# Expert gate weights fetched from DRAM per tile instead of copied in SBUF, and two PSUM banks for tile results

## The chip, the cores and the metric

The kernel runs on one core of one Trainium2 chip. The metric is the time of one execution in microseconds of device time, lower is better. Three runs of the kernel before are given; one further execution was profiled.

## The reference

The input is `x` of shape (16, 256, 128), all in float32. Four blocks follow each other, each adding to `x`; the two mixture-of-experts blocks have the same weights.

```
x = x + attn_a(layernorm(x))      # causal, 16 heads of 8
x = x + ffn(layernorm(x))
x = x + attn_b(layernorm(x))      # scaled by norms, 16 heads
x = x + ffn(layernorm(x))

def ffn(x):                        # D=128, HIDDEN=512, 8 experts, top 2
    logits = flat_x @ Wr
    top_vals, top_idx = top_k(logits, 2)
    rw = softmax(top_vals)
    combine = sum(rw[..., None] * one_hot(top_idx, 8), axis=1)
    g = einsum('nc,ech->neh', flat_x, Wg)
    u = einsum('nc,ech->neh', flat_x, Wu)
    h = silu(g) * u
    eo = einsum('neh,ehc->nec', h, Wd) / sqrt(12)
    out = einsum('ne,nec->nc', combine, eo)
```

## The kernel before

The program is written out by hand for each engine, and semaphores join the five instruction streams; nothing is reordered by a scheduler. Each stream runs attention A, the expert tiles of layer 0, attention B, and the expert tiles of layer 1.

**The expert tiles.** The 4096 tokens, each with two experts, are sorted by expert: a routing step on VectorE gives every (token, choice) pair a row of the DRAM tensor `xg`, in which each expert begins at a multiple of 128 rows. That makes at most `TILES` = 71 tiles of 128 rows per layer. GpSimd scatters the normalised tokens `xn` into `xg` with indirect DMAs (line 1214) and later gathers the results from `eo` (line 1227). The tokens are routed in two groups; the second group's routing and scatters run beside the first tiles, in pieces that `pe_route`, `act_route` and `dve_route` place ahead of tile `k`. The constants `ROUTE_...` say at which `k`: LN at 0, T 1, LG 2, PICK 3, CNT 4, SUM 5, BASE 6, SLOT 7, and two more pieces at 8 and 9. The last one fills the table `te` with the expert of each tile.

**One iteration `k` of `tile_loop`, engine by engine.** TensorE (`pe_tile`): g of tile k (line 1331, four 128x128 matmuls into `psS`), u of tile k (line 1338, into `psT`), the transpose T of tile k+1 (line 1321), y of tile k-1 (line 1350, four matmuls into `psN`). ScalarE (`act_tile`): a copy of the u weights of tile k+1 (`wuc`), silu of g into `sg`, a copy of the transposed tile into `xTt` (line 1366). VectorE (`dve_tile`): the copy of tile k-2's result from `psN` into `ysb` (line 1395), the copy of tile k+1's gate weights into `wgc` (line 1388), the product `hT` of tile k (line 1402). SyncE (`sp_tile`): the load of `xin` for tile k+2 once T of tile k is done (line 1415), the store of `ysb` of tile k-2 (line 1419). A tile's weights lie in SBUF for all eight experts (`wg`, `wu`, `wd`, loaded during attention A); an engine that needs an expert's slice reads its column from `te` into a register first (line 1298, `expert`).

GpSimd makes the `wgc` copies of the first `POOL_COPIES` = 9 tiles of each layer (line 1239), VectorE those of the other 62.

What sets the order around the change is the text of these functions, and the waits in them. `f_sem` counts finished pieces by tile: y of tile k-1 waits for `F_y` of the tile before it, that is for the copy that empties the single bank `psN`:

```
after(pe, f["h"], n0 + k)
if k == 1:
    pe.wait_ge((LA, LB)[l].s["x1"], NBLK)
after(pe, f["y"], n0 + k - 1)
```

The last ten iterations of layer 0 also hold first steps of attention B (`AHEAD_...`). Behind some iterations VectorE combines the gathered results into `x` and starts the next normalisation (`dve_behind`).

## Time and profile before

| | us |
|---|---|
| runs shown: median, lowest, highest | 1279.55, 1272.09, 1284.77 |
| the profiled execution's own time | 1278.22 |
| its span, from first to last instruction | 1276.4 |
| tile loop of layer 0, first to last `xTt` copy | 368.7 to 595.1 |
| tile loop of layer 1, first to last `xTt` copy | 1005.1 to 1221.1 |

Engines are named PE (TensorE matmul), PEld (its weight load, which overlaps), DVE (VectorE), ACT (ScalarE), POOL (GpSimd) and SP (SyncE); a name with a q behind it is that engine's sequencer, and SPq rows are DMA issues. A float32 matmul of 128x128 stands in the rows as two instructions, so the four matmuls of g are x8. "psS<-xTt,wgc" reads: writes psS, reads xTt and wgc. Times count from the span's start. In square brackets stands how long the engine was idle before a row, and what released it.

### The profile page before, as it was taken

To read this page: it belongs to the slowest core of one execution; us is meant where nothing else is said; L and a number is where in the kernel's file an instruction comes from. 1 tells how busy PE (TensorE), PEld (TensorE's weight loads), DVE (VectorE), ACT (ScalarE), POOL (GpSimd) and SP (SyncE) were. 2 spreads that over 40 slices of the span, in tenths; PEclk is the share of its full clock that TensorE was granted. 3 is DMA by queue.
4 is the path that set the end of the run, shared out by engine and by line. 5 is a ranking of instruction groups with operands and counts; after the bars stand their busy time and mean duration, and the time that the engine had idled before them with its cause. 6 is when DMAs were issued, how large, how long until landed. Compare 5 with 4: busy or idle time off the path is not lost.

```text
span 1276.4 us, 29420 instructions
## 1 busy us (share of the span) xinstructions
PE 1067.0 (84%) x9198; PEld 732.0 (57%) x9198; DVE 816.1 (64%) x2452; ACT 673.3 (53%) x1399; POOL 551.6 (43%) x1028
## 2 busy tenths in 40 slices
PE   3988999887788999998788889998867789999940
PEld 1344555443377899887334344443522689999940
DVE  5677778867646445657667888888674464445622
ACT  2465777643433455454276678887645434555520
POOL 2233444325823611444777545454635135014335
PEclk9998999886659999999577799998856789999975
DMA  5585444632101212222433323333201012122222
GB/s 158 118 212 136 102 103 119 172 107 50 39 23 53 83 56 57 72 72 78 109 82 101 81 66 89 89 91 77 52 23 41 22 55 82 55 59 80 72 82 67
DMA packets 163006, 104.80 MB, mean 82 GB/s; under 512 B 15397, under 2 KB 156201, under 8 KB 162857
## 3 DMA queue, kind: packets, MB, share of 16 engines
q1 hardware_dynamic: 154664, 86.14, 26.1%
q0 software_dynamic: 8192, 16.79, 4.6%
q8 instruction: 79, 1.29, 0.5%
q14 instruction: 71, 0.57, 0.2%
HBM read 52.74 MB, written 50.14 MB: 81 GB/s over the span
## 4 chain that ended last, share of the span: by engine, by line
PE 64%; DVE 17%; issue 9%; POOL 3%; ACT 2%; another core or an unknown queue 2%; DMA 2%; SPq 1%; ACTq 0%; DVEq 0%; POOLq 0%
PE psS L1331 10%; PE psT L1338 9%; PE psO L309 8%; PE psN L1350 8%; PE psS L343 7%; DVE mx L655 4%; PE psS L370 3%; PE psT L351 3%; PE psM L267 3%; PE psM L1321 2%; PE psN L316 2%; PE psN L325 1%; PE psO L945 1%; PE psM L410 1%
## 5 line engine op out<-in xcount | busy, mean ns | idle before, releaser
L655 DVE TENSOR_REDUCE mx<-psS 128x3 f32<-128x384 f32 (+1 forms) x512 | 311.9, 617 | 138.5 <-PE psS L370 67.1
L343 PE MATMUL psS<-kst,qst 48*128 48x256 bf16 (+1 forms) x1024 | 205.5, 290 | 57.5 <-DVE mx L655 44.3
L542 ACT ACTIVATE pT<-psT,scb 128x512 f32<-128x512 f32 x256 | 194.7, 778 | 74.0 <-PE psT L351 42.8
L351 PE MATMUL psT<-qst,kst 50*128 50x256 bf16 (+1 forms) x1024 | 198.9, 286 | 9.6 <-ACT pT L542 4.5
L1214 POOL DMA_INDIRECT xg<-xn,slot x128 | 124.0, 969 | 112.8 <-DVE slot L1177 29.5
L1350 PE MATMUL psN<-wd,hT 128*128 x1136 | 153.8, 279 | 18.6 <-DVE ysb L1395 16.6
L1331 PE MATMUL psS<-xTt,wgc 128*128 128x128 f32 x1136 | 157.2, 282 | 12.6 <-ACT xTt L1366 6.9
L771 POOL TENSOR_SCALAR_AFFINE_SELECT pT<-pT 128x256 f32<-128x256 f32 x256 | 103.9, 413 | 142.2 <-ACT pT L537 140.6
L1402 DVE TENSOR_TENSOR hT<-sg,psT 128x512 f32<-128x512 f32 x142 | 97.5, 686 | 105.3 <-PE psT L1338 83.6
L343 PEld LDWEIGHTS psS<-kst,qst 48*128 48x128 bf16 x1024 | 67.4, 97 | 157.9 <-DVE mx L655 79.2
L309 PE MATMUL psO<-pT,vp 128*32 128x256 f32 (+1 forms) x2048 | 152.3, 425 | 5.6 <-POOL pT L771 5.6
L537 ACT ACTIVATE pT<-psT 128x384 f32<-128x384 f32 x256 | 122.5, 490 | 60.4 <-PE psT L351 55.8
L1338 PE MATMUL psT<-xTt,wuc 128*128 128x128 f32 x1136 | 153.3, 279 | 0.0
L1350 PEld LDWEIGHTS psN<-wd,hT 128*128 128x128 f32 x1136 | 139.6, 194 | 23.1 <-issue 22.8
L1331 PEld LDWEIGHTS psS<-xTt,wgc 128*128 128x128 f32 x1136 | 141.9, 196 | 18.8 <-ACT xTt L1366 14.2
L1338 PEld LDWEIGHTS psT<-xTt,wuc 128*128 128x128 f32 x1136 | 141.6, 196 | 0.0
L1375 ACT ACTIVATE sg<-psS 128x512 f32<-128x512 f32 x142 | 84.7, 597 | 102.1 <-PE psS L1331 75.7
L1227 POOL DMA_INDIRECT pT<-eo,slot x64 | 61.2, 956 | 165.2 <-DVE ysb L1395 156.9
L1358 ACT ACTIVATE wuc<-wu 128x512 f32 x142 | 89.4, 630 | 47.7 <-issue 47.5
L309 PEld LDWEIGHTS psO<-pT,vp 128*32 128x32 f32 x2048 | 60.1, 123 | 67.1 <-issue 36.2
L1388 DVE COPY wgc<-wg 128x512 f32 x124 | 54.2, 437 | 53.5 <-issue 45.1
L1227 POOL DMA_INDIRECT xn<-eo,slot x64 | 60.8, 949 | 54.6 <-DMA eo<-ysb 37.1
(210 smaller groups left out, 1542.3 us busy)
## 6 DMA issues: line engine op xcount, KB each, us to landing
scr_part<-part SPq DMA_DIRECT2D x128, 128.0 KB, 2.2
qst<-scr_part SPq DMA_DIRECT2D x64, 192.0 KB, 3.4
kst<-scr_part SPq DMA_DIRECT2D x64, 192.0 KB, 4.4
xin<-xg SPq DMA_DIRECT2D x142, 64.0 KB
eo<-ysb SPq DMA_DIRECT2D x142, 64.0 KB
scr_part<-part SPq DMA_DIRECT2D x32, 192.0 KB, 2.0
xg<-zero SPq DMA_DIRECT2D x7, 576.0 KB, 5.1
scr_part<-part SPq DMA_DIRECT2D x32, 64.0 KB, 2.2
```

The costliest lines, as they stand in the source:

```text
L309: last = nc.tensor.matmul(psO[q // 2][32 * i:32 * i + 32, o0 + dst[0]:o0 + dst[1]], vp[r][:, kb, h, :], pT[:, h % 8, src[0]:src[1]], start ...
L343: return nc.tensor.matmul(ps[:, c0:c0 + n], q_[r64, t, q0], k_[r64, t, 0:n], start=(half == 0), stop=True, skip_group_check=True)
L351: return nc.tensor.matmul(ps[:, c0:c0 + T - q0], k_[m64, t, half * P:half * P + P], q_[m64, t, q0:T], start=True, stop=True, skip_group_ch ...
L537: nc.scalar.activation(pT[:, g % 8, 0:cols], psT[g % 2][:, 0:cols], ACT.Exp, scale=float(HD) ** -0.5).then_inc(s["exp"], 1)
L542: nc.scalar.activation(pT[:, g % 8, 0:cols], psT[g % 2][:, 0:cols], ACT.Exp, scale=scb[r][:, 0, i:i + 1], bias=scb[r][:, 1, i:i + 1]).then ...
L655: nc.vector.tensor_reduce(mx3[:, u, 0:n, pos:pos + 1].rearrange("p a b -> p (a b)"), psS[h % 2][:, 0:kcols(L)].rearrange("p (a k) -> p a k ...
L771: nc.gpsimd.affine_select(out=d, in_=d, compare_op=ALU.is_ge, fill=0.0, base=0, pattern=[[0, 2], [1, P]], channel_multiplier=-1).then_inc( ...
L1214: nc.gpsimd.indirect_dma_start(xg, bass.IndirectOffsetOnAxis(ap=slot[g][:, i, k:k + 1], axis=0), xn[:, BASE[g] + k, :], None).then_inc(r_s ...
L1227: nc.gpsimd.indirect_dma_start(gathered(g, pair), None, eo[0:(OWN, TILES)[g] * P, :], bass.IndirectOffsetOnAxis(ap=slot[g][:, i, k:k + 1], ...
L1331: last = nc.tensor.matmul(psS[p][:, cols], wgc[p][:, cols], xTt[p][:], start=True, stop=True, skip_group_check=True)
L1338: last = nc.tensor.matmul(psT[p][:, cols], wuc[p][:, cols], xTt[p][:], start=True, stop=True, skip_group_check=True)
L1350: last = nc.tensor.matmul(psN[:, 0:P], hT[1 - p][:, hb, :], wd[:, bass.ds(e + hb * P, P)], start=(hb == 0), stop=(hb == HB - 1))
```

## The change

VectorE and GpSimd no longer copy gate weights. In their place SyncE, in `sp_tile` of iteration k, reads the expert of tile k+2 from a new table `te_row` into a register and issues a DMA of that expert's 128x512 block (256 KB) from DRAM into one of three `wgc` buffers; it waits for g of the tile that used the buffer before. The matrix `wg` in SBUF and its preload are gone. Results of tiles go in turn to the banks `psN` and `psO[0]`, so that y of a tile waits for the copy of the tile two before. The tables `te_row` and `te` are made by two more VectorE instructions than `te` alone.

```diff
+FETCH = 3
+        psY = [psN, psO[0]]
-        wg = sb("wg", [P, E * HID])
+        te_row = sb("te_row", [1, TILES], I32)
-        wgc = [sb(f"wgc{i}", [P, HID]) for i in range(2)]
+        wgc = [sb(f"wgc{i}", [P, HID]) for i in range(FETCH)]
+        f_wg = [sem(f"F_wg{i}") for i in range(FETCH)]
...
+            def tables(lo, hi):
+                e = tef[:, lo:hi]
+                link(nc.vector.tensor_scalar(e, e, float(E - 1), float(P), ALU.min, ALU.mult))
+                nc.vector.tensor_copy(te_row[:, lo:hi], e)
+                link(nc.vector.tensor_scalar(tem[:, lo:hi], e, float(HB), None, ALU.mult))
+                nc.vector.tensor_copy(te[:, lo:hi], tem[:, lo:hi]).then_inc(r["slots"], 1)
...
         def pool_ffn(pool, l):
-            pool.wait_ge(r_sem["slots"], 4 * l + 2)
-            for t in range(POOL_COPIES):
-                e = expert(pool, l, t)
-                after(pool, f_sem["g"], n0 + t - 1)
-                nc.gpsimd.tensor_copy(wgc[t % 2][:], wg[:, bass.ds(e, HID)]).then_inc(f_sem["wg"], 1)
...
-                after(pe, f["wg"], n0 + k + 1)
+                after(pe, f_wg[(n0 + k) % FETCH], 16 * ((n0 + k) // FETCH + 1))
...
-                after(pe, f["y"], n0 + k - 1)
+                if k == 2:
+                    pe.wait_ge(r_sem["lg"], LG_COPIES[2 * l + 1] + 1)
+                after(pe, f["y"], n0 + k - 2)
                 for hb in range(HB):
-                    last = nc.tensor.matmul(psN[:, 0:P], hT[1 - p][:, hb, :], wd[:, bass.ds(e + hb * P, P)],
+                    last = nc.tensor.matmul(psY[1 - p][:, 0:P], hT[1 - p][:, hb, :], wd[:, bass.ds(e + hb * P, P)],
...
         def dve_tile(dve, l, k, p):
-                e = expert(dve, l, t)
-                after(dve, f["wg"], n0 + t)
-                after(dve, f["g"], n0 + t - 1)
-                nc.vector.tensor_copy(wgc[p][:], wg[:, bass.ds(e, HID)]).then_inc(f["wg"], 1)
-                nc.vector.tensor_copy(ysb[p][:], psN[:, 0:P]).then_inc(f["y"], 1)
-            if live(k, 1):
-                weights(k + 1, 1 - p)
+                nc.vector.tensor_copy(ysb[p][:], psY[p][:, 0:P]).then_inc(f["y"], 1)
...
+        def sp_gate(sp, l, t):
+            n = l * TILES + t
+            if t == EARLY:
+                sp.wait_ge(r_sem["slots"], 4 * l + 4)
+            row0 = sp.value_load(te_row[0:1, t:t + 1], min_val=0, max_val=(E - 1) * P)
+            after(sp, f_sem["g"], n - FETCH + 1)
+            sp.dma_start(wgc[n % FETCH][:], A["L0_ffn_Wg"].rearrange("e c h -> (e c) h")[bass.ds(row0, P), :]
+                         ).then_inc(f_wg[n % FETCH], 16)
...
                 sp.dma_start(xin[p][:], xg[row0:row0 + P, :]).then_inc(f_ld[p], 16)
+                sp_gate(sp, l, k + 2)
...
+            sp.wait_ge(r_sem["slots"], 4 * l + 2)
+            for t in range(2):
+                sp_gate(sp, l, t)
             dispatched(0)
```

On SyncE, at the start of layer 0's tiles, before: the last steps of attention A, the first `xin` loads, and then loads and stores in turn.

```order
L811 DMA scr_m<-mrow 8x512 [waits A_mrow,A_m2]
L814 DMA qst<-scr_m 2x4x256 [waits A_mscr]
L814 DMA qst<-scr_m 2x4x256
L1411 DMA xin<-xg 128x128 [waits R_scat0]
L1411 DMA xin<-xg 128x128
L1415 DMA xin<-xg 128x128 [waits F_T_ps] x3
L1419 DMA eo<-ysb 128x128 [waits F_y]
```

The same place now (iteration 2's fetch, of tile 4, and the first store stand at its end):

```order
L1404 DMA wgc<-in_L_ffn_Wg 128x512
L1413 DMA xin<-xg 128x128 [waits R_scat0]
L1413 DMA xin<-xg 128x128
...
L1417 DMA xin<-xg 128x128 [waits F_T_ps]
L1402 TENSOR_LOAD te_row
L1402 ISA x2
L1404 ISA [waits F_g]
L1404 DMA wgc<-in_L_ffn_Wg 128x512
L1422 DMA eo<-ysb 128x128 [waits F_y]
```

The first two fetches stand ahead of the wait for the scatters (`R_scat0`); every later one stands between a load of `xin` and a store of `eo`.

On VectorE, at the end of the last routing piece (k = 9) and the tile behind it, before:

```order
L1206 TENSOR_SCALAR tef<-tef 1x46 [waits s_chain]
L1207 CAST te<-tef 1x46 [waits s_chain]
L1395 COPY ysb<-psN 128x128 [waits F_st1,F_y_ps]
L1298 TENSOR_LOAD te
L1298 ISA x2
L1388 ISA [waits F_g,F_wg]
L1388 COPY wgc<-wg 128x512
L1402 TENSOR_TENSOR hT<-sg,psT 128x512 [waits F_y_ps,F_u,F_silu]
```

and now:

```order
L1192 TENSOR_SCALAR tef<-tef 1x46 [waits s_chain]
L1193 CAST te_row<-tef 1x46 [waits s_chain]
L1194 TENSOR_SCALAR tem<-tef 1x46
L1195 CAST te<-tem 1x46 [waits s_chain]
L1389 COPY ysb<-psO 128x128 [waits F_st1,F_y_ps]
L1394 TENSOR_TENSOR hT<-sg,psT 128x512 [waits F_y_ps,F_u,F_silu]
```

The register load, the wait for g and the copy between `ysb` and `hT` are gone, two short instructions stand ahead of them, and the result comes from the other bank.

## Rows read from the trace of the kernel before

**Rows 1.** The page: busy time of each engine with its share of the span

```profile
PE 1067.0 (84%) x9198; PEld 732.0 (57%) x9198; DVE 816.1 (64%) x2452; ACT 673.3 (53%) x1399; POOL 551.6 (43%) x1028
```

**Rows 2.** Busy time by stretch, layer 0: length, engines, clock, DMA share, GB/s

```profile
463.00:527.00 64.00, 64.00 (x576) 64.00 (x575) 34.14 (x78) 34.55 (x69) 11.89 (x13) 1.00 0.22 60
```

**Rows 3.** Timeline of one quiet tile of layer 0: start, length, engine, what

```profile
456.25 0.27 PE L1321 MATMUL psM<-ident,xin 128*128 128x128 f32 x1
...
456.56 0.32 SPq L1415 DMA_DIRECT2D xin<-xg  x1
...
457.73 1.06 PE L1331 MATMUL psS<-xTt,wgc 128*128 128x128 f32 x8
457.93 0.29 DVE L1395 COPY ysb<-psN 128x128 f32<-128x128 f32 x1 [0.74 <-PE psN L1350]
...
458.74 0.43 DVE L1388 COPY wgc<-wg 128x512 f32 x1 [0.52 <-issue]
```

**Rows 4.** Timeline of PE beside the routing: layer 0, then one of layer 1

```profile
384.72 0.27 PE L1321 MATMUL psM<-ident,xin 128*128 128x128 f32 x1
386.33 1.15 PE L1350 MATMUL psN<-wd,hT 128*128 x8 [1.34 <-DVE ysb L1395]
...
405.41 0.27 PE L1321 MATMUL psM<-ident,xin 128*128 128x128 f32 x1
407.21 1.15 PE L1350 MATMUL psN<-wd,hT 128*128 x8 [1.53 <-issue]
...
1041.84 1.15 PE L1350 MATMUL psN<-wd,hT 128*128 x8 [1.60 <-DVE ysb L1395]
```

**Rows 5.** Timeline of DVE beside the routing of layer 0

```profile
389.53 0.69 DVE L1402 TENSOR_TENSOR hT<-sg,psT 128x512 f32<-128x512 f32 x1 [1.15 <-PE psT L1338]
...
399.96 0.69 DVE L1402 TENSOR_TENSOR hT<-sg,psT 128x512 f32<-128x512 f32 x1 [0.53 <-PE psT L1338]
...
403.02 0.43 DVE L1388 COPY wgc<-wg 128x512 f32 x1 [0.79 <-issue]
...
406.70 0.27 DVE L1395 COPY ysb<-psN 128x128 f32<-128x128 f32 x1
```

**Rows 6.** Timeline of PE, the other waits for ysb: layer 0, last of layer 1

```profile
534.69 1.15 PE L1350 MATMUL psN<-wd,hT 128*128 x8 [1.25 <-DVE ysb L1395]
...
578.16 1.15 PE L1350 MATMUL psN<-wd,hT 128*128 x8 [1.39 <-DVE ysb L1395]
...
603.79 2.07 PE L1350 MATMUL psN<-wd,hT 128*128 x8 [4.27 <-DVE ysb L1395]
...
1225.23 1.15 PE L1350 MATMUL psN<-wd,hT 128*128 x8 [0.57 <-DVE ysb L1395]
```

**Rows 7.** Timeline, end of layer 0's tiles: the last ysb copy

```profile
605.90 0.29 DVE L1395 COPY ysb<-psN 128x128 f32<-128x128 f32 x1 [2.35 <-PE psN L1350]
```

**Rows 8.** DMA issues: queue, KB each, us from issue to landing; then line L1488

```profile
wg<-in_L_ffn_Wg SPq DMA_DIRECT2D x4, 512.0 KB, 5.0
...
wd<-in_L_ffn_Wd SPq DMA_DIRECT2D x8, 256.0 KB, 4.0
...
DMA to landing us min/median/max: 3.6/5.1/6.9
```

**Rows 9.** Line L1298, register loads: duration ns min/median/max, first and last start

```profile
L1298 DVEq TENSOR_LOAD <-te x124: 298/303/550, 401.9 to 1219.2; - x124
L1298 DVEq FUSED_REGOPS  x124: 190/190/206, 402.5 to 1219.6; - x124
```

**Rows 10.** Timeline beside the second group's scatters, layer 0; then line L1214

```profile
421.84 0.27 PE L1321 MATMUL psM<-ident,xin 128*128 128x128 f32 x1
...
422.78 0.28 ACT L1366 ACTIVATE xTt<-psM 128x128 f32<-128x128 f32 x1 [1.04 <-PE psM L1321]
...
451.25 0.28 ACT L1366 ACTIVATE xTt<-psM 128x128 f32<-128x128 f32 x1 [1.04 <-PE psM L1321]
...
L1214 POOL DMA_INDIRECT xg<-xn,slot x128: 952/958/1245, 298.3 to 1088.4; - x128
```

More of the change, by code:

```diff
@@ L199, in build @@
         r_gat = [sem(f"R_gat{q}") for q in range(NBLK // 4)]
-        f_sem = {n: sem("F_" + n) for n in ["T_ps", "xT", "wg", "wu", "g", "u", "silu", "h", "y_ps", "y"]}
+        f_sem = {n: sem("F_" + n) for n in ["T_ps", "xT", "wu", "g", "u", "silu", "h", "y_ps", "y"]}
         f_ld = [sem(f"F_ld{i}") for i in range(2)]
+        f_wg = [sem(f"F_wg{i}") for i in range(FETCH)]
         f_st = [sem(f"F_st{i}") for i in range(2)]
@@ L1205, in dve_route_part @@
                     link(nc.vector.tensor_tensor(out=late, in0=late, in1=tem[:, EARLY:], op=ALU.add))
-                link(nc.vector.tensor_scalar(late, late, float(E - 1), float(HID), ALU.min, ALU.mult))
-                nc.vector.tensor_copy(te[:, EARLY:], late).then_inc(r["slots"], 1)
+                tables(EARLY, TILES)
         def pool_scatter(pool, n, pair):
@@ L1330, in pe_tile @@
                     cols = slice(hb * P, (hb + 1) * P)
-                    last = nc.tensor.matmul(psS[p][:, cols], wgc[p][:, cols], xTt[p][:],
+                    last = nc.tensor.matmul(psS[p][:, cols], wgc[(n0 + k) % FETCH][:, cols], xTt[p][:],
                                             start=True, stop=True, skip_group_check=True)
@@ L1380, in dve_tile @@
             f, n0 = f_sem, l * TILES
-            def weights(t, p):
-                if t < POOL_COPIES:
-                    return
-                e = expert(dve, l, t)
-                after(dve, f["wg"], n0 + t)
-                after(dve, f["g"], n0 + t - 1)
-                nc.vector.tensor_copy(wgc[p][:], wg[:, bass.ds(e, HID)]).then_inc(f["wg"], 1)
-            if k == 0:
-                weights(0, 0)
             if live(k, -2):
@@ L1521, in hook @@
                     if h == 14:
-                        pe.wait_ge(s_wffn, 16 * 17)
+                        pe.wait_ge(s_wffn, 16 * 13)
                         pe.wait_ge(s_half, 4)
```

12 lines of the change are left out of this document (4 added, 8 removed).

## The prediction

> **What bounds the kernel now.** I read the page first: TensorE is busy 84% of the span, VectorE 64% [rows 1]. That is a mean over attention, which the change hardly touches, and the two tile loops, so I went to the stretches. In a quiet part of the first loop TensorE is busy for all of 64.00 us while VectorE has 34.14 [rows 2]: 64 us hold 576 matmul instructions, 25 to a tile (8 each for g, u, y and one T), so a tile takes 64 x 25 / 576 = 2.78 us, and the spacing of the `xTt` copies there is 2.79. In that stretch a copy less on VectorE is worth nothing, since VectorE waits for TensorE. The first loop, with 70 steps from 368.7 to 595.1, takes 226.4 us where 70 x 2.79 is 195.3; the second takes 216.0. So 31 and 21 us are lost to something else, and the change can only win there. The timeline of TensorE says where. Beside the routing, y stands idle in front of `psN` because VectorE, busy with a routing piece, has not yet emptied it: 1.34 us at 386.33, 1.53 at 407.21, and 1.60 at the matching place of layer 1 [rows 4]. Later the same wait returns at 534.69, 578.16, 603.79 and 1225.23 [rows 6]. Those waits, not the copies, are what the second bank removes.
>
> **Part 1, the second bank.** Beside layer 0's routing, from T of tile 4 to T of tile 10, TensorE needs 405.41 - 384.72 = 20.69 us for six tiles [rows 4]; six periods are 16.74, so 3.95 too many, and the wait of y at 407.21 adds 1.53. The two matmuls of the counts are real work of about 0.2. That leaves 5.3 to be won if VectorE keeps up. Does it? y of a tile needs its own `hT`, and `hT` still stands behind the routing piece; the second bank only lets TensorE run some two microseconds further ahead of a heavy piece and spend it on the light ones. VectorE's work from the `hT` at 389.53 to the `ysb` copy at 406.70 is 17.17 us; less its wait of 0.53, and less the wgc copy with the issue ahead of it (0.79 + 0.43), 15.4 remain [rows 5]. The table costs two more short instructions, an estimate of 0.4 from neighbours of some 0.2 each: 15.8. With the wait at 386.33 gone, that `hT` starts at about 388.15, and `ysb` of tile 7 comes at 388.15 + 15.8 = 404.0, the `hT` behind it ends at 404.9. TensorE, at 2.79 a tile from 384.85 with the counts' 0.2, reaches that y at 384.85 + 0.2 + 7 x 2.79 = 404.6. VectorE is 0.3 late: I take 5.0 for layer 0. Layer 1 has the same pieces, and its wait of 1.60 [rows 4]: 5.0 again.
>
> At 534.69 and 578.16 the `ysb` copy stood behind a root of the normalisation and behind the scaled tokens of attention B; `hT` of the tile was ready both times, so 1.25 and 1.39 go [rows 6]. At 603.79 the chain changes more: y of tile 70 waited 4.27 for the copy of tile 69. With two banks it runs at once, but attention B waits for the copy of tile 70, and that can't start before VectorE is through with the copy of tile 69, so what is won is VectorE's own wait, 2.35 [rows 7], not 4.27. In layer 1 the last one gives 0.57 [rows 6]; behind it comes a tail of gathers that only moves up by this. Sum: 5.0 + 5.0 + 1.25 + 1.39 + 2.35 + 0.57 = **15.6 us**.
>
> **Part 2, the copies that go.** 124 copies on VectorE at 0.43 us with 0.52 of issue ahead [rows 3], and 18 on GpSimd, go. I price them at nothing beyond what stands above: in the quiet tiles TensorE covers them wholly [rows 2]. If that cover were gone they would be worth up to 0.95 x 124 = 118 us, which the busy share excludes.
>
> **Part 3, the fetch.** It adds 142 transfers of 256 KB. The question is the way from T of tile k to g of tile k+2. T is seen at 456.56, when SyncE issues `xin` [rows 3]. Then come that issue (0.32), the register load (0.30) and its arithmetic (0.19) [rows 9]; SyncE has no such row, so VectorE's stand in. Landing counts from the issue of the DMA. The nearest rows are the 256 KB of `wd` at 4.0 and the 512 KB of `wg` from the same rows of DRAM at 5.0 [rows 8]. I take 4.0, for it has the size. So the weights are there at 456.56 + 0.8 + 4.0 = 461.4. g of that tile stands at 457.73 [rows 3], two tiles on is 463.3. That is 1.9 us in hand: hidden. At the worst landing of the 512 KB loads, 6.9 [rows 8], it is 1.0 late; below nothing it can't go, since g doesn't start before T and y. The fetch's wait for g of tile k-1 has always passed, for T of tile k stands behind it on TensorE. Queued behind the fetch on SyncE are the store of `ysb` (0.5 to 0.9 later; the next writer of that buffer is two tiles off) and the next load of `xin`, which has nearly two tiles. In the routing stretch SyncE is itself held by late `ysb` copies, so a fetch or two will reach TensorE some 0.5 late: I charge 1.0 in all, between 0 and 4. At the loop's start the fetches of tiles 0 and 1 stand ahead of the wait for the scatters, while SyncE is idle, and cost nothing. The preload of `wg` (four loads of 512 KB beside attention A) goes, worth between 0 and 1; I take 0. The two table instructions in the first groups' routing lie in attention, where VectorE is on the path: 0.4 x 2 = 0.8.
>
> What VectorE's register load shows is 303 ns [rows 9]. The Trainium skill (DMA: Bandwidth & Descriptors, Latency and other measured facts) gives a `tensor_load` a floor of about 600 ns; by the page the slack would be 1.6 instead of 1.9, and the trace does not agree with it.
>
> **The sum.** 15.6 - 1.0 - 0.8 = 13.8 us. Against the profiled execution's own 1278.2 us (its span is 1276.4) that makes 1264.4; this execution lies 1.3 below the median of 1279.55, well inside the runs' own spread. Forecast: **1264 us**, own range 1259 to 1270.
>
> **Rival A, the fetch comes late, slower than before.** The DMA queues carry 60 GB/s in the quiet stretch [rows 2]. With the fetch a tile moves 384 KB, 138 GB/s at 2.79 us, and one and a half gathers of 64 KB add 34, so some 170, which no tile of the trace has. If the landing there is 6.9 [rows 8], the weights miss g by 1.0, and as each fetch is released two tiles ahead, a tile loses 0.5. It decides at a landing of 5.9. Over some 60 tiles with GpSimd's DMAs beside them that costs 30 us: 1278.2 - 13.8 + 30 = 1294. For it: that untried traffic. Against it: the 6.9 belongs to transfers of twice the size, and in the scatter stretch tiles already take 3.16, which gives 0.7 more slack.
>
> **Rival B, VectorE and SyncE take TensorE's place.** My sum lets VectorE come within 0.3 us of TensorE at the end of the routing. Should its pieces not close up, because their chain waits, or because `xin` and fetches stand behind late stores on SyncE, each layer keeps only its first waits, some 2 us instead of 5.0, and attention B starts no earlier because its own operands set it (2.35 lost): 1264.4 + 3 + 3 + 2.3 = 1272.7. For it: the 0.3. Against it: each row of DVE in this stretch but two starts without waiting.
>
> **Rival C, GpSimd's DMAs get faster.** Beside GpSimd's scatters, T at 421.84 is seen by ScalarE only at 422.78, 0.94 after its start [rows 10], where SyncE sees it after 0.31 in a quiet tile [rows 3]; nine such tiles, from 422.78 to 451.25, take 3.16 us each [rows 10]. If VectorE's copies have a part in it, the 0.37 over some 20 such tiles goes as well: 7.5 us, so 1257. Against it: the indirect DMAs take 952 ns at the least and 958 in the median [rows 10], so hardly any is held up. The Trainium skill (SBUF — State Buffer, "SBUF: two separate sides") says that a float32 SBUF-to-SBUF copy on VectorE locks GpSimd out of a shared port, so that it can't write its descriptors. The flat durations do not bear that out for most of them; by that rule this rival's 7.5 us would come.
>
> **How the numbers follow.** Forecast 0.50, rival A 0.15 (1294), rival B 0.23 (1273), rival C 0.12 (1257). A measurement of this kernel can tell about 1%, that is 12.8 us, from no change, so the line stands at 1266.8. Of the forecast's half, 0.37 lies below it and 0.13 above. Faster: 0.37 + 0.12 = 0.49, taken as 0.5; within 1%: 0.13 + 0.23 = 0.36, taken as 0.35; slower: 0.15. The range reaches from below rival C to the milder half of A: 1252 to 1289.
>
> **What would show it.** Right: in the profile after, y has no idle of note behind `ysb` at tiles 2 to 10; T of tile 10 follows T of tile 4 by 17 us instead of 20.69; the quiet tiles stay at 2.79; g has no wait for `wgc`; the fetch lands in about 4. Wrong in the way of A: idle of g ended by a DMA, tiles of 3.2 us or more beside the gathers. Wrong in the way of B: `hT` late, y idle behind it. Wrong in the way of C: the tiles beside the scatters below 3.16. The forecast falls as a whole if the waits for `ysb` go but each is followed by one of the same length for another releaser.

## The result and the profile after

The changed kernel takes 1270.41 us in the median of 20 runs (1263.43 to 1275.89), the kernel before 1278.04 beside it (20 runs, 1269.28 to 1288.64). The ratio is 0.9947, with a 95% interval of 0.9924 to 0.9969: 6.8 us, or 0.5%, faster. The sign of the forecast was right, the size was not: 13.8 us had been forecast, and the bound of 1% was not reached. The profiled execution of the changed kernel took 1263.43 us and is the fastest of its 20, so that its own lead of 14.8 us says too much; below I compare lengths of stretches inside the tile loops, which have their period of 2.79 us in every run.

The page of the changed kernel, engines and three groups (out<-in, count, busy and mean ns, idle before and its releaser), answers to [rows 1]:

```profile
PE 1053.7 (84%) x9198; PEld 729.3 (58%) x9198; DVE 761.0 (60%) x2336; ACT 671.6 (53%) x1399; POOL 541.6 (43%) x1010
...
L1221 POOL DMA_INDIRECT xg<-xn,slot x128 | 124.5, 973 | 174.9 <-DVE ysb L1389 79.7
...
L1234 POOL DMA_INDIRECT pT<-eo,slot x64 | 60.8, 950 | 167.8 <-DMA eo<-ysb 104.0
...
L1354 PE MATMUL psN<-wd,hT 128*128 x576 | 77.5, 278 | 1.2 <-DVE hT L1394 0.6
```

VectorE has 55 us less to do (816.1 to 761.0). y, which had stood idle for 1.3 to 1.6 us at a time beside the routing [rows 4], has 1.2 us of idle time left in all 576 matmuls that go to `psN`, the half of y shown here, and 0.3 in the 560 that go to `psO`. T of tile 10 follows T of tile 4 by 17.0 us (398.11 after 381.14), as forecast. So the wait that the second bank was to remove is gone. The windows of the changed kernel say the same; the first window is the routing of layer 0, the second answers to [rows 2]:

```profile
381.00:395.60 14.60, 14.60 (x133) 14.58 (x132) 12.45 (x53) 7.57 (x16) 0.00 (x0) 1.00 0.46 136
463.00:527.00 64.00, 63.09 (x564) 62.71 (x563) 25.23 (x61) 33.55 (x68) 14.21 (x15) 1.00 0.58 155
```

TensorE is busy in all of the 14.60 us beside the routing. In the long window it now lacks 0.9 us, though VectorE has less work; g waits 0.24 and 0.66 us for `xTt` at steps 42 and 50, beside gathers, of the kind shown further below.

A quiet tile of the changed kernel (timeline), beside [rows 3]:

```profile
457.69 0.27 PE L1323 MATMUL psM<-ident,xin 128*128 128x128 f32 x1
...
457.99 0.32 SPq L1417 DMA_DIRECT2D xin<-xg  x1
...
458.89 0.29 DVE L1389 COPY ysb<-psO 128x128 f32<-128x128 f32 x1 [0.26 <-PE psO L1354]
459.06 0.35 SPq L1404 DMA_DIRECT2D wgc<-in_L_ffn_Wg  x1
459.45 0.43 SPq L1422 DMA_DIRECT2D eo<-ysb  x1
```

The fetch leaves 1.07 us after `xin` (0.8 was reckoned), and the store of `ysb` follows it, 0.56 us after the copy began. Windows of half a microsecond behind this fetch show when it lands (the last figure of a row is GB/s):

```profile
460.00:460.50 0.50, 0.50 (x7) 0.50 (x6) 0.00 (x0) 0.38 (x1) 0.00 (x0) 1.00 1.01 102
460.50:461.00 0.50, 0.50 (x7) 0.50 (x6) 0.27 (x1) 0.21 (x1) 0.00 (x0) 1.00 0.67 217
461.00:461.50 0.50, 0.50 (x7) 0.50 (x7) 0.42 (x1) 0.14 (x2) 0.00 (x0) 1.00 0.92 316
461.50:462.00 0.50, 0.50 (x7) 0.50 (x6) 0.29 (x1) 0.50 (x1) 0.00 (x0) 1.00 0.35 101
```

In the half microsecond before them 1 GB/s passes. These 2 us hold the weights (256 KB), the store behind them (64 KB) and most of the next `xin`; its rest passes by 462.2. So the weights are there at most 2.9 us after their issue at 459.06, where I had taken 4.0. In windows of 0.1 us the first 328 KB, as much as weights and store together, end at 461.6, which makes it 2.5. No g waits for them here.

**Where the gain went.** I count steps: a step is the time from one `xTt` copy to the next, 2.79 us when nothing holds TensorE. The tables give three stretches of each loop.

| us | steps 3 to 25 | steps 26 to 69 | loop, 70 steps |
|---|---|---|---|
| layer 0, before | 77.59 | 135.28 | 226.46 |
| layer 0, changed | 75.67 | 133.35 | 222.04 |
| layer 1, before | 79.95 | 124.46 | 216.07 |
| layer 1, changed | 75.96 | 126.71 | 214.05 |

Steps count from 0, so step 10 ends with the `xTt` copy of tile 11. Up to step 9 the changed kernel has won what was forecast: steps 4, 6 and 7 of layer 0 were 4.55, 3.57 and 4.07 us long and are 3.01, 2.79 and 2.79. By the start of step 10 it is 5.7 us ahead in layer 0, counted from the loop's start. Then step 10 takes 8.12 us where it took 4.20 at step 9 and 5.00 at step 10 before; in layer 1 step 10 takes 8.15 us. The timeline of the changed kernel at that step:

```profile
400.56 0.96 POOL L1221 DMA_INDIRECT xg<-xn,slot  x1 [0.30 <-issue]
...
400.90 0.27 PE L1323 MATMUL psM<-ident,xin 128*128 128x128 f32 x1
...
403.67 0.60 ACT L1379 ACTIVATE sg<-psS 128x512 f32<-128x512 f32 x1 [3.98 <-remote]
404.36 0.96 POOL L1221 DMA_INDIRECT xg<-xn,slot  x1 [0.30 <-issue]
406.53 0.32 SPq L1417 DMA_DIRECT2D xin<-xg  x1
406.54 0.28 ACT L1370 ACTIVATE xTt<-psM 128x128 f32<-128x128 f32 x1 [2.27 <-remote]
...
406.87 0.58 PE L1333 MATMUL psS<-xTt,wgc 128*128 128x128 f32 x1 [4.80 <-ACT xTt L1370]
```

T has run at 400.90, and ScalarE and SyncE, which see it after 0.3 us in a quiet tile, both go on only at 406.53. Two engines that have nothing to do with each other are released in the same moment, 1.2 us after GpSimd's last scatter of a row has ended (404.36 + 0.96). That row has seven indirect DMAs without a pause, from 396.42; before, it had six, from 402.79. Completions can also be seen inside the row: g had ended at 400.17, and silu (`sg`) started on it at 403.67, 3.5 us later. Behind the hold the clock falls as well (the column after POOL is the granted clock):

```profile
401.00:406.60 5.60, 1.06 (x10) 0.87 (x8) 0.04 (x1) 0.66 (x2) 3.40 (x4) 0.87 0.44 124
406.60:411.00 4.40, 4.13 (x19) 4.13 (x20) 1.10 (x3) 1.54 (x4) 1.99 (x3) 0.50 0.42 123
```

After 4.8 us without a matmul TensorE gets 0.50 of full speed, the 1.2 GHz level, in the next 4.4 us.

**Theory 1** came from this: a row of indirect DMAs on GpSimd holds TensorE's completions until it has ended; TensorE that is further ahead when the slots are ready makes the row longer, and so the second bank pays its gain back. **Theory 2**: the fetch's traffic costs what the bank wins. **Theory 3**: VectorE's or SyncE's chain takes TensorE's place. **Theory 4** came up on the way: GpSimd's 32 scatters of a layer, one every 1.26 us, become the bound, since the second group's first tile needs the last of them.

The later runs fell on five chips, and they are of two kinds. The kernel before takes 1275.5 us on one of them (the kind of the first measurement, 1278.0; **kind 1**) and 1228.6 to 1231.6 on four (**kind 2**). Each chip was used at one time only, so whether the kind belongs to the chip or to its condition at that time is not shown. Each ratio below is against the kernel before on the same chip, and the kind stands with each run. Steps are read from one profiled execution of each kernel.

### The profile page after: what moved, and what is told of

Its sections match the earlier page's. It is cut to its first block, busy times and chain, and to the rows that moved or that the text cites. A ratio compares the mean times of both kernels' runs of the same rounds, so it can differ in the third digit from the quotient of the medians.

```text
span 1261.7 us, 29444 instructions
## 1 busy us (share of the span) xinstructions
PE 1053.7 (84%) x9198; PEld 729.3 (58%) x9198; DVE 761.0 (60%) x2336; ACT 671.6 (53%) x1399; POOL 541.6 (43%) x1010
## 4 chain that ended last, share of the span: by engine, by line
PE 64%; DVE 14%; issue 9%; another core or an unknown queue 3%; ACT 3%; POOL 3%; DMA 2%; SPq 1%; ACTq 0%; DVEq 0%; POOLq 0%
PE psS L1333 11%; PE psT L1340 9%; PE psO L312 8%; PE psS L346 7%; PE psN L1354 4%; DVE mx L658 4%; PE psO L1354 4%; PE psS L373 3%; PE psT L354 3%; PE psM L270 2%; PE psN L319 2%; PE psM L1323 2%; PE psO L947 1%; PE psN L328 1%
## 5 line engine op out<-in xcount | busy, mean ns | idle before, releaser
L354 PE MATMUL psT<-qst,kst 50*128 50x256 bf16 (+1 forms) x1024 | 196.1, 283 | 11.0 <-DMA qst<-scr_m 3.9
L312 PE MATMUL psO<-pT,vp 128*32 128x256 f32 (+1 forms) x2048 | 146.7, 412 | 8.6 <-POOL pT L774 8.2
L1234 POOL DMA_INDIRECT pT<-eo,slot x64 | 60.8, 950 | 167.8 <-DMA eo<-ysb 104.0
L1354 PE MATMUL psN<-wd,hT 128*128 x576 | 77.5, 278 | 1.2 <-DVE hT L1394 0.6
L373 PE MATMUL psS<-trib,identb 128*128 128x256 bf16 x256 | 78.1, 305 | 0.0
L1370 ACT ACTIVATE xTt<-psM 128x128 f32<-128x128 f32 x142 | 39.3, 277 | 70.4 <-PE psM L1323 62.1
```

What stands on the lines that cost most here:

```text
L312: last = nc.tensor.matmul(psO[q // 2][32 * i:32 * i + 32, o0 + dst[0]:o0 + dst[1]], vp[r][:, kb, h, :], pT[:, h % 8, src[0]:src[1]], start ...
L354: return nc.tensor.matmul(ps[:, c0:c0 + T - q0], k_[m64, t, half * P:half * P + P], q_[m64, t, q0:T], start=True, stop=True, skip_group_ch ...
L373: last_s = nc.tensor.matmul(psS[par][:, 0:3 * P].rearrange("p (a k) -> p a k", a=3)[:, 0:3:2, :], identb[:], trib[:].unsqueeze(1).to_broad ...
L1234: nc.gpsimd.indirect_dma_start(gathered(g, pair), None, eo[0:(OWN, TILES)[g] * P, :], bass.IndirectOffsetOnAxis(ap=slot[g][:, i, k:k + 1], ...
L1354: last = nc.tensor.matmul(psY[1 - p][:, 0:P], hT[1 - p][:, hb, :], wd[:, bass.ds(e + hb * P, P)], start=(hb == 0), stop=(hb == HB - 1))
```

## The experiments

### The bank alone, the fetch alone

```diff
 # bank_only: the kernel before, with
+        psY = [psN, psO[0]]
-                after(pe, f["y"], n0 + k - 1)
+                if k == 2:
+                    pe.wait_ge(r_sem["lg"], LG_COPIES[2 * l + 1] + 1)
+                after(pe, f["y"], n0 + k - 2)
 # fetch_only: the changed kernel, with
-        psY = [psN, psO[0]]
+        psY = [psN, psN]
-                after(pe, f["y"], n0 + k - 2)
+                after(pe, f["y"], n0 + k - 1)
```

> The kernel before with the second PSUM bank for the tile results alone; gate weights are copied on chip as before. Theory 1 (what the bank wins beside the routing is taken back by a hold of TensorE's completions while GpSimd issues a row of scatters without a pause): the steps beside the routing are short as in the changed kernel (no wait for the ysb copy), one long step of 7 to 8 us follows in each layer at the first second-group scatters, and the time is 4 to 8 us under the kernel before. Theory 2 (the fetch's DMA traffic, 28 GB/s more over the span, costs what the bank wins): this kernel keeps the whole forecast gain, 13 to 16 us under the kernel before. Theory 3 (the bank's second semaphore distance moves the wait to VectorE or SyncE and wins nothing itself): within 2 us of the kernel before.

> The changed kernel with its tile results in one bank again: the fetch alone. Theory 1: the fetch is nearly free, within 3 us of the kernel before, and the steps beside the routing wait for the ysb copy again. Theory 2: 6 to 9 us slower than the kernel before, spread over the tiles' steps. Theory 3: 5 to 7 us faster, since the copies that went are the whole gain.

> The second bank alone once more, for the kind of chip that it falls on. On a chip where the kernel before takes some 1276 us, theory 1: one long step at each layer's row of scatters as in the changed kernel, and 3 to 7 us under the kernel before; theory 2: 13 us and more under it.

> The fetch alone, tile results in one bank. On the first kind of chip theory 1 expects 0 to 3 us under the kernel before, with the waits for the ysb copy beside the routing left and the step at the first row of scatters between the 4 to 7 us of the kernel before and the 8 us of the changed one; theory 2 expects it 3 us or more over the kernel before. On the second kind 3 to 5 us under it, as measured once.

All four fell on kind 2. The bank alone: 1223.68 against 1231.62, ratio 0.9947 (0.9928 to 0.9967), and 1226.25 against 1228.56, ratio 0.9958 (0.9928 to 0.9989). The fetch alone: 1227.33 against 1231.62, ratio 0.9976 (0.9953 to 0.9999), and 1228.37 against 1231.52, ratio 0.9972 (0.9946 to 0.9997). So the bank is worth 5.2 to 6.5 us and the fetch 3.0 to 3.4: here the fetch is not a cost but a gain, and theory 2 falls on this kind. The bank's number lies in the range that theory 1 gave, by luck: the long step of 7 to 8 us that was to come with it is absent. The steps say what happened. Steps 4 to 10 of layer 0 sum to 25.29 us in the kernel before of kind 2 (label before_3), 24.18 with the fetch alone, 23.12 with the bank alone, and 19.77 with both (after_3). Each alone wins 1 to 2 us of this stretch, both together 5.5. The reason stands in the timeline of the bank alone, TensorE and VectorE:

```profile
399.90 1.13 PE L1332 MATMUL psS<-xTt,wgc 128*128 128x128 f32 x8 [1.02 <-issue]
404.53 1.13 PE L1332 MATMUL psS<-xTt,wgc 128*128 128x128 f32 x8 [1.60 <-issue]
...
399.38 0.43 DVE L1391 COPY wgc<-wg 128x512 f32 x1 [0.79 <-issue]
...
403.86 0.57 DVE L1391 COPY wgc<-wg 128x512 f32 x1 [0.53 <-issue]
```

g stands idle for 1.02 and 1.60 us until VectorE, late with its routing pieces, has copied the gate weights: with the bank alone the wait for `ysb` becomes a wait for `wgc` (399.38 + 0.43 and 403.86 + 0.57, each followed by g within 0.1 us). With the fetch alone y waits for `ysb` as before:

```profile
400.85 1.15 PE L1352 MATMUL psN<-wd,hT 128*128 x8 [1.47 <-DVE ysb L1387]
```

### The changed kernel and the kernel before, again

> The changed kernel itself once more, beside the bank alone and the fetch alone of the first call, which ran on a chip where the kernel before takes 1231.6 us. Theory 1 (a row of scatters without a pause holds TensorE's completions): on such a chip its scatters follow each other without a pause for 20 and more, and no step beside them was held, so the long step of 8.1 us is absent. Theory 4 (new: GpSimd's 32 scatters of a layer, 1.26 us from one to the next, become the bound; they can't start before the slots are there and the first of the second group's tiles needs the last of them): steps 24 and 25 of each layer, 2.8 us before, take 4.5 to 5.5 us each, and the time is 8 to 10 us under the kernel before, less than the 12.2 that bank alone (7.9) and fetch alone (4.3) give when added. If neither holds, the sum of both, 12 us or more, is seen.

> The kernel before, for its profile on the same chip. Theory 1 expects long steps of 4 us and more only where the scatters form a row of 6 or more, as in the first trace (steps 9 to 11). Theory 4 expects the last scatter of the layer to be issued over 2 us ahead of the tile that needs it, steps 24 and 25 at 2.8 us.

> The changed kernel again. On a chip where the kernel before takes 1228 to 1232 us, theory 1: no row of scatters holds TensorE there, so the gain is the forecast's, 11 to 15 us (ratio 0.988 to 0.991). Theory 4 (the 32 scatters of a layer are the bound there): 6 to 9 us, with steps 25 and 26 of each layer 3.5 to 5 us long. On a chip of the first kind: 5 to 8 us as measured twice.

> The kernel before for its profile beside these. On the second kind of chip theory 1 expects its steps 14 to 22 at 2.79 us, not the 3.16 of the first trace, and the waits for the ysb copy beside the routing (steps 4, 6, 7) as in the first trace.

Kind 1: 1269.1 against 1275.5, ratio 0.9953 (0.9921 to 0.9985), the first result once more. Step 10 takes 6.75 us in layer 0 and 8.10 in layer 1. In layer 0 the row of scatters has eight DMAs, from 398.62, and the hold ends inside it (after_again, TensorE, then GpSimd and ScalarE):

```profile
403.09 0.27 PE L1323 MATMUL psM<-ident,xin 128*128 128x128 f32 x1
...
406.54 0.96 POOL L1221 DMA_INDIRECT xg<-xn,slot  x1 [0.30 <-issue]
407.36 0.28 ACT L1370 ACTIVATE xTt<-psM 128x128 f32<-128x128 f32 x1 [2.32 <-remote]
...
407.80 0.95 POOL L1221 DMA_INDIRECT xg<-xn,slot  x1 [0.31 <-issue]
```

T is seen 4.3 us after its start, while the seventh DMA runs and the eighth is still to come. So theory 1 as I put it, a hold until the row has ended, is too strong: the longer row has the shorter step.

Kind 2: 1218.83 against 1229.26, ratio 0.9927 (0.9898 to 0.9956), 9.0 us faster. That is at the upper end of what theory 4 expected and below theory 1's 11 to 15, whose lower edge the interval (5.4 to 12.5) still holds. Bank and fetch apart sum to 8.2 to 9.9, the same as together, so that the whole times don't show the surplus that steps 4 to 10 have.

On kind 2 a row of scatters holds nothing. The changed kernel there (after_3), GpSimd and then ScalarE at steps 10 and 11:

```profile
397.37 1.31 POOL L1221 DMA_INDIRECT xg<-xn,slot  x1 [37.75 <-DVE ysb L1389]
...
402.77 0.95 POOL L1221 DMA_INDIRECT xg<-xn,slot  x1 [0.30 <-issue]
...
399.38 0.28 ACT L1370 ACTIVATE xTt<-psM 128x128 f32<-128x128 f32 x1 [0.41 <-PE psM L1323]
402.17 0.28 ACT L1370 ACTIVATE xTt<-psM 128x128 f32<-128x128 f32 x1 [0.41 <-PE psM L1323]
404.95 0.28 ACT L1370 ACTIVATE xTt<-psM 128x128 f32<-128x128 f32 x1 [0.41 <-PE psM L1323]
```

The scatters follow each other every 1.26 us and are as long as on kind 1, and `xTt` comes every 2.79 us, after an idle 0.41 of ScalarE. In the kernel before (before_3) the steps beside the scatters, 3.16 us on kind 1 [rows 10], are 2.79 here. The instructions are the same and take the same time; what differs is when TensorE's completions are seen.

What is lost on kind 2 stands at the end of the scatters. The first tile of the second group may be loaded only when the last scatter has landed (after_3, GpSimd's last scatter, SyncE, TensorE):

```profile
436.87 0.96 POOL L1221 DMA_INDIRECT xg<-xn,slot  x1 [0.30 <-PE psT L1340]
...
433.86 0.32 SPq L1417 DMA_DIRECT2D xin<-xg  x1
439.12 0.32 SPq L1417 DMA_DIRECT2D xin<-xg  x1
...
443.39 0.43 SPq L1417 DMA_DIRECT2D xin<-xg  x1
...
445.58 0.33 PE L1323 MATMUL psM<-ident,xin 128*128 128x128 f32 x1 [0.38 <-DMA xin<-xg]
446.53 1.15 PE L1354 MATMUL psN<-wd,hT 128*128 x8 [0.61 <-DVE hT L1394]
```

`xin` comes 5.26 us after the last one, and SyncE, which now has three DMAs a tile to catch up with, reaches the one that T at 445.58 needs too late. Steps 25 and 26 take 3.72 and 3.66 us; in the kernel before SyncE has the same pause and catches up with both steps at 2.79. In layer 1 it is 3.37 and 2.79. This is theory 4 in a small form: 0.6 to 1.8 us a layer, where it had expected 3 us and more. Another 1.0 us goes at steps 12 and 13: VectorE's `ysb` copy at 407.29 stands idle for 1.69 us until the eo store of the tile two before, issued at 402.98, has landed; in between SyncE's issue of the next store takes 1.48 us instead of 0.43.

### Without the scatters of the second group

```diff
-                pool_scatter(pool, 2 * l + 1, pair)
+                pass
-                for q in range(G):
-                    pool.wait_ge(r_scat[q], 16 * 2 * SIZE[q] * (n // G + 1))
+                pool.wait_ge(r_scat[0], 16 * 2 * SIZE[0] * (n // G + 1))
-                if k == EARLY - 2:
-                    dispatched(1)
```

> The changed kernel with the second group's scatters left out (its tokens are never written into the tiles' rows, and the tiles don't wait for them). Theories 1 and 4 both: the steps from 9 to 26 are 2.8 us each with no long one, and the time is 8 to 14 us under the changed kernel. Theory 2 (the fetch's traffic costs what the bank wins): the steps beside the fetches stay as they are, and the time falls by under 3 us.

> The kernel before without the second group's scatters, likewise left out. Theories 1 and 4: the changed kernel's lead over this pair is the forecast's 13 to 16 us, since nothing takes the bank's gain back. Theory 2: the lead stays 5 to 9 us. The waits for the ysb copy beside the routing stay in this kernel.

Both leave the second group's rows unwritten and the waits for them out. Both fell on kind 1, beside after_again. 1242.6 (ratio 0.9742, 0.9711 to 0.9773) and 1260.69 us (ratio 0.9904, 0.9869 to 0.9938) against 1275.5. Leaving the scatters out wins 26.5 us in the changed kernel and 14.8 in the kernel before; the lead of the changed kernel grows from 6.4 to 18.1 us. Theory 2 had expected a fall of under 3 us and a lead of 5 to 9. But 26.5 is also far over the 8 to 14 us that theories 1 and 4 expected; in the profiled executions the two loops account for 19.8 of it. Step 10, 6.75 us in after_again, is 2.79 here, like its neighbours (after_noscat, ScalarE):

```profile
400.45 0.28 ACT L1369 ACTIVATE xTt<-psM 128x128 f32<-128x128 f32 x1 [0.41 <-PE psM L1322]
403.24 0.28 ACT L1369 ACTIVATE xTt<-psM 128x128 f32<-128x128 f32 x1 [0.41 <-PE psM L1322]
```

Steps 3 to 25, in us, and the lead of the changed kernel in them:

| | before | changed | lead |
|---|---|---|---|
| kind 1, first pair, layers 0 and 1 | 77.59, 79.95 | 75.67, 75.96 | 1.9, 4.0 |
| kind 1, second pair | 76.13, 76.99 | 73.90, 76.89 | 2.2, 0.1 |
| kind 1, no second-group scatters | 69.65, 69.74 | 65.05, 64.59 | 4.6, 5.2 |
| kind 2 | 69.92, 70.04 | 66.34, 65.79 | 3.6, 4.3 |

The lead of 4.6 and 5.2 us is the forecast's 5.0 for each layer. With the scatters kind 1 keeps 0.1 to 4.0 of it, kind 2 3.6 and 4.3. The lead in time of 18.1 us is more than the 9.4 us by which the two loops of this pair differ, and more than the forecast; both medians are of few runs (4 and 5), and the lead carries their spread. I take the steps as the firmer number. Leaving the scatters out also removes the wait for the last of them, which on kind 1 too makes step 25 longer in the changed kernel than before (3.70 and 3.27 us in layer 0 of the first pair, 4.24 and 2.79 in layer 1 of the second); so part of the returned lead, 0.4 to 1.5 us a layer over the two pairs, is not the row's.

### Scatters held back

```diff
+        def late(pair):
+            return max(0, 2 - pair // 8)
-                    pool.wait_ge(f_sem["y"], n0 + ROUTE_SLOT - 1 + pair // 2)
+                    pool.wait_ge(f_sem["y"], n0 + ROUTE_SLOT - 1 + late(pair) + pair // 2)
 # and the same in the wait for f_sem["u"]
```

> The changed kernel, with the first eight second-group scatters of each layer held for two more tiles, the next eight for one more, so that GpSimd doesn't issue the first ones in a row. Theory 1: the long step at their start (8.1 us in each layer) falls to 3 to 4 us, and the time is 5 to 9 us under the changed kernel. Theory 2 and 3: the scatters' order doesn't matter, or the long step is a wait for routing data and stays: within 2 us of the changed kernel.

> The same two waits in the kernel before, where the row of scatters without a pause is 6 long and the longest step is 4.2 us in layer 0 and 7.2 us in layer 1. Theory 1: the time falls by 3 to 6 us, less than in the changed kernel. Theories 2 and 3: within 2 us of the kernel before.

Both fell on kind 2. The changed kernel with it: 1224.87 against 1231.62, ratio 0.9955 (0.9927 to 0.9984), no better than without on the other chip (0.9927). The kernel before with it: 1241.05, ratio 1.0088 (1.0061 to 1.0115), 10.8 us slower by the ratio. Theory 1 expected a gain from a hold that this kind doesn't have, so it could not be tested; what the pair shows is theory 4. GpSimd needs 32 times 1.26, 40.4 us, for a layer's scatters, and tiles 9 to 24 take TensorE 16 times 2.79, 44.6 us: there is little room. With the scatters begun late, steps 24 and 25 of layer 0 take 5.72 and 6.14 us in the changed kernel and 5.73 and 5.19 in the kernel before.

### Rows of indirect DMAs beside quiet tiles

```diff
+        SPARE = (((27, "dma", 1), (29, "dma", 2), (31, "dma", 3), (34, "dma", 6)),
+                 ((27, "copy", 1), (29, "copy", 6), (32, "dma", 4), (35, "dma", 2)))
 # in pool_ffn, between the scatters and the gathers
+            for t, kind, count in SPARE[l]:
+                pool.wait_ge(f_sem["y"], n0 + t)
+                # count copies of 128x512, or count indirect DMAs of one block to a spare tensor
```

> The changed kernel with extra work on GpSimd alone in the quiet tiles, none of it used: in layer 0 rows of 1, 2, 3 and 6 indirect DMAs of 64 KB to a spare tensor, in layer 1 one copy and six copies of 128x512, then rows of 4 and 2 indirect DMAs. Theory 1: one or two DMAs cost no step more than 0.4 us, three cost about 1 us, four some 2 us, six some 4 to 5 us (as far as the row outlasts the step), and seven copies of the same length cost nothing. Theory 2 (traffic): all rows cost the same per byte, 64 KB beside the tile's 384, so under 0.5 us each. On a chip of the kind with 1232 us for the kernel before, theory 1 expects no hold at all.

> The changed kernel with rows of 1, 2, 3 and 6 unused indirect DMAs (layer 0), then one and six copies, four and two indirect DMAs (layer 1) on GpSimd beside quiet tiles. On the first kind of chip theory 1: rows of 1 and 2 and the copies cost under 0.4 us, three about 1 us, four about 2, six about 5. Theory 2 (traffic): under 0.5 us for each row. On the second kind nothing, as its first run showed.

> The changed kernel with rows of 1, 2, 3 and 6 unused indirect DMAs (layer 0, tiles 27 to 38), then one and six copies, four and two indirect DMAs (layer 1). If it falls on a chip of the first kind, theory 1: rows of 1 and 2 and the copies cost under 0.4 us, three about 1 us, four about 2, six about 5; theory 2 (traffic): under 0.5 us for each row. On the second kind nothing, as twice before.

All three fell on kind 2, with one run each: 1216.18, 1213.7 and 1218.65 us, no slower than the changed kernel there. A row of six and the tiles beside it (after_rows_2, GpSimd, then a window over the rows of two, three and six of layer 0):

```profile
469.50 0.95 POOL L1262 DMA_INDIRECT spare<-xn,slot  x1 [4.89 <-DVE ysb L1409]
...
475.80 0.96 POOL L1262 DMA_INDIRECT spare<-xn,slot  x1 [0.30 <-issue]
...
454.09:484.77 30.68, 30.68 (x277) 30.68 (x276) 10.76 (x23) 16.54 (x33) 10.52 (x11) 1.00 0.58 168
```

TensorE is busy for all of the 30.68 us, at 168 GB/s. On kind 2 a row of any length up to six costs nothing, nor do the copies of layer 1: every step beside them is 2.79. What it costs on kind 1 was not measured by itself; no run of this kernel fell there.

### More traffic, and another order on SyncE

```diff
 # after_double, in sp_gate: a second, unused fetch of 256 KB
+            sp.dma_start(spare[n % FETCH][:], A["L0_ffn_Wu"].rearrange("e c h -> (e c) h")[bass.ds(row0, P), :]
+                         ).then_inc(f_spare[n % FETCH], 16)
 # after_eo_first, in sp_tile: the eo store of tile k-2 ahead of the gate fetch of tile k+2
-                sp_gate(sp, l, k + 2)
             if live(k, -2):
                 ...
                 sp.dma_start(eo[row0:row0 + P, :], ysb[p][:]).then_inc(f_st[p], 16)
+            if live(k, 2):
+                sp_gate(sp, l, k + 2)
```

> The changed kernel with a second, unused 256 KB fetch behind each gate fetch. Theory 2 (the fetch's traffic or its issue costs what the bank wins): 6 to 9 us slower than the changed kernel, so at or above the kernel before. Theory 1: only the issue on SyncE counts, 0.35 us of a queue that is idle for most of a 2.79 us tile; it makes the eo store later by as much once more, so 0 to 3 us slower than the changed kernel, and all of that in the gathers' steps.

> The changed kernel with SyncE's eo store put ahead of the gate fetch in each tile. Theory 1 (a row of three or more indirect DMAs on GpSimd holds TensorE's completions for a step; the store queued behind the fetch comes up to 0.9 us later, so that the first gather starts late and the gathers come in threes): the 3.4 to 4.1 us steps among tiles 42 to 62 of each layer get fewer, and on a chip where the kernel before takes some 1276 us it is 3 to 6 us under the changed kernel, 9 to 12 under the kernel before. On a chip where rows hold nothing (the kernel before takes some 1232 us) no gain beyond 1 us. Theory 3 (the gathers wait for the ysb copy in either case): within 1 us of the changed kernel.

Both fell on kind 2. Twice the fetch: 1229.9 against 1228.56, ratio 0.9992 (0.9954 to 1.003); beside the 0.9927 of the changed kernel that is some 8 us lost, across chips. The size is theory 2's for this run, though a single fetch costs nothing in the runs above. Most of it is lost beside the scatters: steps 3 to 25 are 4.7 and 3.8 us longer than in after_3, steps 26 to 69 1.4 and 1.8. In the quiet tiles TensorE is busy throughout at 250 GB/s (after_double, VectorE beside the scatters, then a window):

```profile
403.19 0.29 DVE L1391 COPY ysb<-psO 128x128 f32<-128x128 f32 x1 [1.54 <-DMA eo<-ysb]
...
463.00:527.00 64.00, 64.00 (x576) 64.00 (x575) 28.05 (x76) 34.46 (x70) 17.02 (x18) 1.00 0.83 250
```

The `ysb` copies wait for the landing of the store two tiles back, which stands behind both fetches on SyncE. One such wait stands in after_3 too, at steps 12 and 13. So one fetch is near the point where this begins, and two are past it.

The store ahead of the fetch: 1230.85 against 1228.56, ratio 1.0014 (0.9989 to 1.0039), so the whole gain of the change is lost, beside the 0.9927 of the changed kernel on another chip. Now the fetch stands behind SyncE's wait for `ysb`, which is late beside the routing (after_eo_first, SyncE, then TensorE):

```profile
393.40 0.35 SPq L1404 DMA_DIRECT2D wgc<-in_L_ffn_Wg  x1
393.79 1.48 SPq L1417 DMA_DIRECT2D xin<-xg  x1
...
396.64 1.13 PE L1333 MATMUL psS<-xTt,wgc 128*128 128x128 f32 x8 [1.58 <-issue]
```

g stands idle for 1.58 us and goes 3.24 us after the fetch that it needs was issued; steps 5, 8 and 11 of layer 0 take 3.85, 4.61 and 4.33 us. This is the forecast's rival A, brought about by an order in a queue. My expectation had not seen it.

### Gathers one tile later and never three in a row

```diff
-                pool.wait_ge(f_sem["y"], n0 + OWN + 2 * pair // 3 + 1)
+                pool.wait_ge(f_sem["y"], n0 + OWN + 2 * pair // 3 + 2)
+                if pair % 3 == 1:
+                    pool.wait_ge(f_sem["u"], n0 + OWN + 2 * pair // 3 + 4)
```

> The changed kernel with the first group's gathers one tile later, and the second gather of a tile held until half a tile after the first, so that no three come in a row. Theory 1, first kind of chip: the steps of 3.4 to 4.3 us among tiles 42 to 62 fall to 3.1 at most, 3 to 6 us under the changed kernel. Second kind: within 1 us of it. Theory 3: the later gathers delay the sums on VectorE and the time grows by 1 to 3 us on both.

Kind 2: 1223.56 against 1229.26, ratio 0.9952 (0.9923 to 0.998); the changed kernel beside it had 0.9927. Its median is 4.7 us above the changed kernel's, 10 runs against 6, but the two intervals overlap (0.9923 to 0.9956), so a loss is likely and not shown; it would be theory 3's side. On kind 2 there is nothing for it to win. The steps that it was meant for exist on kind 1 alone, in after_again for instance, GpSimd and ScalarE:

```profile
499.93 0.97 POOL L1234 DMA_INDIRECT pT<-eo,slot  x1 [52.62 <-DMA eo<-ysb]
501.21 0.96 POOL L1234 DMA_INDIRECT pT<-eo,slot  x1 [0.30 <-issue]
502.47 0.94 POOL L1234 DMA_INDIRECT pT<-eo,slot  x1 [0.31 <-issue]
...
499.30 0.28 ACT L1370 ACTIVATE xTt<-psM 128x128 f32<-128x128 f32 x1 [0.41 <-PE psM L1323]
502.78 0.28 ACT L1370 ACTIVATE xTt<-psM 128x128 f32<-128x128 f32 x1 [1.09 <-PE psM L1323]
```

The step is 3.48 us long. In layer 1 the kernel before has one such step of 4.4 us among tiles 42 to 62 (before_again), the changed kernel five of 3.8 to 4.0 (after_again), each followed by one of 2.53. This is why it loses 2.3 and 3.3 us in steps 26 to 69 of layer 1 in the two pairs of kind 1, and 0.4 on kind 2. The first gather now waits for the landing of the eo store (104.0 us on the page), which is issued behind the fetch. That the lateness of this store makes the threes was only argued: before_noscat, which has no fetch, shows three of them in layer 1 as well (4.14, 4.44 and 4.00 us).

## Why the prediction was wrong

**The step that failed** is the sum's first two terms, "5.0 for layer 0" and "5.0 again" for layer 1, taken as won to the end. The working inside the stretch was right: where nothing follows, steps 3 to 25 lead by 4.6 and 5.2 us (no second-group scatters). What I left out is what is late next. Behind the routing stand 32 scatters, which the routing releases, and TensorE's earlier arrival meets them. On kind 1 the changed kernel keeps 1.9 and 4.0, or 2.2 and 0.1 us: beside a row of seven or eight scatters one step takes 6.75 to 8.15 us in each layer, followed by a stretch at half clock in the trace shown. In the kernel before the longest step there was 5.00 to 7.23 us. The trace of before had the warning in it: T seen only 0.94 us after its start beside the scatters [rows 10] was used for rival C alone, as something that the change might cure, not as something that it could make longer.

**The later waits.** 1.25 and 1.39 us, 2.6 in all, were forecast for layer 0's later steps; steps 26 to 69 are 1.9 us shorter on kind 1 and 1.6 on kind 2 (130.71 to 129.10), somewhat less. The 2.35 at the end of layer 0 can't be read apart from attention B: from the last `xTt` of layer 0 to the first of layer 1 it is 3.0 us less on kind 2 (387.67 to 384.68), with the 0.4 of the table in it, but 5.2 and 11.4 less in the two pairs of kind 1 and 1.6 more without the scatters. These single executions scatter by more than the term, so no run here shows it. The 0.57 at the end of layer 1 can't be seen behind the gathers' new steps, 2.3 and 3.3 us on kind 1, which no term of the sum held.

**The copies that go**, priced at nothing, are worth more in company: with one bank the fetch wins 3.0 to 3.4 us. The bank without it wins 2.2 us of steps 4 to 10 in each layer on kind 2, for VectorE's `wgc` copy then takes the place of the `ysb` copy. My 5.0 had subtracted the copy from VectorE's work, so the sum was right for both, but "worth nothing" was not.

**The table.** Its two more instructions cost VectorE 0.33 us beside the routing (0.89 from the `tensor_scalar` to the `ysb` copy, 0.56 before), where 0.4 was estimated; what the ones in attention cost in time no run here shows by itself.

**The fetch.** Landing 4.0 forecast, at most 2.9 measured; the charge of 1.0 for late fetches was not paid in the way I put it: beside the routing no g waits for a fetch, and only in step 25 of layer 1 on kind 1 does one stand idle for 0.34 and 0.33 us, 3.0 us after its fetch left. SyncE's queue was paid instead: 0.6 to 1.8 us at steps 25 and 26, 1.0 at steps 12 and 13, on kind 2.

**The rivals.** A did not come in the changed kernel (quiet tiles 2.79 us, 155 GB/s), but its mechanism is real: it takes one move in SyncE's queue to bring it (after_eo_first). B, 1273, is nearest to the measured number and yet not what happened: the pieces on VectorE did close up, and step 9 is 2.79. C fell: with the copies gone the scatters take 973 ns in the mean, where they took 969, and the tiles beside them 3.07 to 3.13 us in layer 0, where they took 3.16; GpSimd's DMAs were no faster. So the shared port that, by the Trainium skill (SBUF — State Buffer, "SBUF: two separate sides"), a float32 copy on VectorE locks against GpSimd's descriptors is not what made these tiles long: the copies went and the tiles stayed.

**What stays open.** Shown: the second-group scatters take back the gain on kind 1 (leaving them out returns the lead of steps 3 to 25 to 4.6 and 5.2 us), and such rows hold nothing on kind 2. Argued, not shown: that it is the row's length that sets the hold, against which the row of eight with 6.75 us speaks, and that GpSimd's issue of these DMAs, and not their traffic or landing, is what delays TensorE's completions. The run that would price a row of known length fell three times on kind 2. What makes a chip of one kind or the other no run here tells. In the profiled executions the loops' own lead is 6.4 us in the first pair on kind 1, near the whole 6.8, but 1.2 in the second, where the medians differ by 6.4; the rest lies outside the loops and has no account.

## What to carry to other kernels

Ask of every wait that is removed what stands next in the program and what released it: here a queue of 32 DMAs on GpSimd, released by the same routing, took the gain back, and its last landing sets the floor for the tiles behind it. A stall often has two engines' late work behind it; taking one away hands the wait to the other (2.2 us for the bank alone, 1.1 for the fetch alone, 5.5 for both in one stretch), so changes that look separate must be priced together. A DMA added to a queue costs what is queued behind it, and moved behind a wait it costs more: the same fetch is nearly free in one place of SyncE's order and costs the whole gain in another.

## What the runs showed of the hardware

- Two kinds of chip: the same kernel takes 1275.5 to 1278.0 us on one and 1228.6 to 1231.6 on the other. In two profiled executions 20.8 us of the difference lie in the two tile loops (224.93 and 212.83 against 212.54 and 204.43 us) and 26.2 between them (413.85 against 387.67). One chip of the first kind and four of the second were seen after the first measurement.
- On the first kind TensorE's completions are seen late beside GpSimd's indirect DMAs: T is seen 0.94 us after its start with two in a row (0.3 in a quiet tile), 5.6 us with seven, and 4.3 with eight. With the seven, ScalarE, SyncE and VectorE are released within 0.03 us, 1.2 us after the row's end; with the eight, while the seventh still runs. On the second kind 32 nearly without a pause hold nothing. The DMAs themselves take 0.96 us, one every 1.26, on both.
- A fetch of 256 KB with a register offset landed at most 2.9 us after its issue in a quiet tile, beside two transfers of 64 KB, and 3.2 us after it where g waited for it in after_eo_first. The register load ahead of it took SyncE 270 ns in the median. A DMA issue on SyncE that mostly takes 0.32 to 0.43 us took 1.48 now and then.
- After 4.8 us without a matmul the granted clock was at 0.50, the 1.2 GHz level, in the next 4.4 us (changed kernel, 406.6 to 411.0).
